# A graph layer pair on one core: TensorE's order within a step is changed, and drains carry its signals

## The reference

```python
def conv(x, W1, W2, src, dst, n):
    deg_out = clip(segment_sum(1, src), 1.0); deg_in = clip(segment_sum(1, dst), 1.0)
    norm = rsqrt(deg_out[src] * deg_in[dst])
    msg = (x[src] @ W1 + x[src] * x[dst] @ W2) * norm[:, None]
    return x @ W1 + segment_sum(msg, dst)
h = relu(conv(x, W1_1, W2_1))
h = conv(h, W1_2, W2_2)
out = layernorm(x + h)
```

## Time and profile before

| | |
|---|---|
| time, median of 3 runs | 1490.88 us (1488.17 to 1492.55) |
| span of the profiled execution | 1516.6 us (1.7% over the median of the runs) |
| mean granted TensorE clock in it | 0.757 of full speed |
| busy: PE / DVE / ACT / POOL | 998.5 / 978.8 / 741.3 / 795.9 us (66 / 65 / 49 / 52% of the span) |
| layer 0 / layer 1 in the span | steps from about 156 to 806 us / from 808 to 1515 us |

### The profile page before, as it was taken

The page is one execution under the profiler, slowest core; times in us unless marked ns, Lnnn a source line. Parts: engine busy times, 40 slices in busy tenths (PEclk is TensorE's granted clock), DMA queues, the critical chain, the costliest instruction groups (busy, mean ns, idle before and its releaser), DMA issues. The chain is left out here.

```text
span 1516.6 us, 33831 instructions
## 1 busy us (share of the span) xinstructions
PE 998.5 (66%) x13162; PEld 933.6 (62%) x13162; DVE 978.8 (65%) x2390; ACT 741.3 (49%) x2763; POOL 795.9 (52%) x813
## 2 busy tenths in 40 slices
PE   1775467666667666766783466767777667776676
PEld 1664356666666656766782366666666666666676
DVE  8577667565556655666583257767677767777676
ACT  3113145555555555655691145545554545555455
POOL 6575435555555555556205655655655555555540
PEclk9999567777777777667796667777787677777776
DMA  9854111122112211212112123333333233323322
GB/s 209 167 217 167 18 32 50 42 52 52 44 47 51 52 50 40 51 51 52 41 52 79 39 58 63 73 69 71 73 70 69 55 72 69 69 58 71 70 58 48
DMA packets 148693, 105.09 MB, mean 69 GB/s; under 512 B 115769, under 2 KB 128761, under 8 KB 147837
## 3 DMA queue, kind: packets, MB, share of 16 engines
q1 hardware_dynamic: 123176, 71.17, 17.8%
q0 software_dynamic: 25216, 32.50, 11.9%
q10 hardware_dynamic: 212, 0.42, 0.1%
HBM read 58.92 MB, written 45.11 MB: 69 GB/s over the span
## 5 line engine op out<-in xcount | busy, mean ns | idle before, releaser
L849 POOL DMA_INDIRECT c_rows<-table,k_row_i x394 | 380.3, 965 | 356.1 <-PE c_sum L882 159.7
L908 PE MATMUL c_out<-k_wcat,c_uvt 128*128 128x64 f32 x1516 | 319.6, 398 | 346.8 <-ACT c_uvt L990 309.5
L908 PEld LDWEIGHTS c_out<-k_wcat,c_uvt 128*128 128x128 f32 x1516 | 303.3, 306 | 373.3 <-ACT c_uvt L990 224.3
L849 POOL DMA_INDIRECT k_rows<-table,k_row_i x346 | 334.1, 966 | 294.5 <-PE c_sum L882 160.8
L990 ACT ACTIVATE c_uvt<-c_turn 128x512 f32<-128x512 f32 (+1 forms) x198 | 106.9, 590 | 539.2 <-remote 512.1
L1200 DVE TENSOR_TENSOR c_sum<-c_sum,c_own 128x512 f32<-128x512 f32 (+1 forms) x96 | 66.7, 695 | 381.9 <-remote 358.8
L882 PE MATMUL c_sum<-c_rows,c_sel 128*128 128x64 bf16 x4701 | 219.6, 221 | 48.2 <-issue 29.8
L882 PEld LDWEIGHTS c_sum<-c_rows,c_sel 128*128 128x128 bf16 x4701 | 219.3, 119 | 52.1 <-issue 50.3
L1141 DVE TENSOR_SCALAR c_sel<-k_place,k_grid 128x512 bf16<-128x512 f16 (+1 forms) x788 | 238.7, 371 | 0.0
L882 PE MATMUL c_sum<-c_yr,c_sel 128*128 128x64 bf16 x1567 | 209.6, 220 | 5.9 <-issue 4.4
L882 PE MATMUL c_sum<-c_rest,c_sel 128*128 128x64 bf16 x1567 | 207.8, 220 | 1.0 <-issue 1.0
(11 more groups left out here) (210 smaller groups left out, 1231.6 us busy)
## 6 DMA issues: line engine op xcount, KB each, us to landing
table<-c_y SPq DMA_DIRECT2D x47, 384.0 KB
out<-c_y SPq DMA_DIRECT2D x47, 256.0 KB
c_res<-in_x SPq DMA_DIRECT2D x46, 256.0 KB
table<-k_xh SPq DMA_DIRECT2D x4, 1820.0 KB
c_rows<-table,k_row_i POOLq DMA_INDIRECT x394
k_rows<-table,k_row_i POOLq DMA_INDIRECT x346
table<-k_xh SPq DMA_DIRECT2D x1, 3575.0 KB
table<-k_xh SPq DMA_DIRECT2D x1, 1040.0 KB
```

Source lines behind the costliest of these rows:

```text
L849: nc.gpsimd.indirect_dma_start(out=rows[:, b % RING, i], out_offset=None, in_=tables[l], in_offset=bass.IndirectOffsetOnAxis(ap=k.row_i[:, ...
L908: last = nc.tensor.matmul(out_bank(g)[:, n, :], uvt[:, g % 2, n, :], weights, start=True, stop=True)
```

## The change

TensorE's step becomes sums of s, transposes of group s - 1, product of group s - 2, counts. The consumers of the product move one step later on each engine: relu from s - 2 to s - 3, the split of its result (`rests`) from s - 3 to s - 4, centre from s - 2 to s - 3, vary and square from s - 3 to s - 4, deviate and normalize from s - 4 to s - 5, the stores from s - 3 - l to s - 4 - l. ACT's `turned_back` moves from the last place of step s to the first place of step s + 1, which is the same place in its queue. The ends of the layers are written out to match. Each increment that rode on the last matmul of a run in `add_up`, `count`, `multiply` and `turn_over` now rides on a drain of TensorE that follows the run. The matmuls of the degree lookups (L864), the lane transposes (L857) and the tally (L921) keep theirs.

```diff
-                for g in ended(s - 3 - l):
+                for g in ended(s - 4 - l):
                     store(g)
...
                         for q, part in enumerate(parts(b)):
-                            last = nc.tensor.matmul(p_sum[g % BANKS][:, t - GROUP[g][0], :], sel[:, b % 2, i, n * P:(n + 1) * P], part[:, i],
+                            nc.tensor.matmul(p_sum[g % BANKS][:, t - GROUP[g][0], :], sel[:, b % 2, i, n * P:(n + 1) * P], part[:, i],
                                                     start=first and q == 0, stop=q == 2, skip_group_check=True)
                     if i == BATCH[b] - 1 or i % HALF_BATCH == HALF_BATCH - 1:
-                        last.then_inc(summed, 1)
+                        pe.drain().then_inc(summed, 1)
...
-                last.then_inc(counted, 1)
+                pe.drain().then_inc(counted, 1)
...
-                last.then_inc(multiplied, 1)
+                pe.drain().then_inc(multiplied, 1)
...
-                last.then_inc(turned, 1)
+                pe.drain().then_inc(turned, 1)
...
                 if s == 1 and l == 0:
                     pe.wait_ge(k.lanes_back, EARLY)
-                for g in ended(s - 2):
-                    multiply(g, turn)
                 add_up(s, turn)
                 for g in ended(s - 1):
                     turn_over(g, turn)
+                for g in ended(s - 2):
+                    multiply(g, turn)
                 if s in COUNT_AT[l]:
                     count(COUNT_AT[l][s], turn)
...
             for s in STEPS:
+                for g in ended(s - 2):
+                    turned_back(g)
                 if l == 1:
-                    for g in ended(s - 3):
+                    for g in ended(s - 4):
                         square(g)
-                    for g in ended(s - 4):
+                    for g in ended(s - 5):
                         deviate(g)
                 for g in ended(s - 1):
                     scale(g)
...
                 if l == 0:
-                    for g in ended(s - 2):
+                    for g in ended(s - 3):
                         relu(g)
                 else:
-                    for g in ended(s - 4):
+                    for g in ended(s - 5):
                         normalize(g)
...
-                for g in ended(s - 1):
-                    turned_back(g)
+            turned_back(g0 - 1)
...
                 if l == 0:
-                    for g in ended(s - 3):
+                    for g in ended(s - 4):
                         rests(g)
...
                 if l == 1:
+                    for g in ended(s - 4):
+                        vary(g)
                     for g in ended(s - 3):
-                        vary(g)
-                    for g in ended(s - 2):
                         centre(g)
```

More of the change, by code:

```diff
@@ L831, in sync @@
                             fetch(g)
-                for g in ended(s - 3 - l):
+                for g in ended(s - 4 - l):
                     store(g)
-            for g in range(g0 - 2 - l, GROUPS):
+            for g in range(g0 - 3 - l, GROUPS):
                 store(g)
@@ L892, in count @@
                 for i in range(b - a):
-                    last = nc.tensor.matmul(k.p_count[:, 0:TILES], hot_l[:, :, i], hot_t[:, i], start=u == COUNTS[0][0] and i == 0,
+                    nc.tensor.matmul(k.p_count[:, 0:TILES], hot_l[:, :, i], hot_t[:, i], start=u == COUNTS[0][0] and i == 0,
                                             stop=True, skip_group_check=True)
-                last.then_inc(counted, 1)
+                pe.drain().then_inc(counted, 1)
             def multiply(g, turn=None):
@@ L907, in multiply @@
                 for n in range(wide(g)):
-                    last = nc.tensor.matmul(out_bank(g)[:, n, :], uvt[:, g % 2, n, :], weights, start=True, stop=True)
-                last.then_inc(multiplied, 1)
+                    nc.tensor.matmul(out_bank(g)[:, n, :], uvt[:, g % 2, n, :], weights, start=True, stop=True)
+                pe.drain().then_inc(multiplied, 1)
             def turn_over(g, turn=None):
@@ L915, in turn_over @@
                 for n in range(wide(g)):
-                    last = nc.tensor.transpose(turn_bank(g, n)[:, n % 4, :], uv[:, g % 2, n].rearrange("p a d -> p (a d)"), k.ident[:, :])
-                last.then_inc(turned, 1)
+                    nc.tensor.transpose(turn_bank(g, n)[:, n % 4, :], uv[:, g % 2, n].rearrange("p a d -> p (a d)"), k.ident[:, :])
+                pe.drain().then_inc(turned, 1)
             def tally():
@@ L1061, in scalar @@
                     A(root_up[:, :], k.degree[:, 8 * LOOKUPS[s]:8 * LOOKUPS[s] + 8], ACT.Sqrt).then_inc(k.root_found, 1)
-                for g in ended(s - 1):
-                    turned_back(g)
+            turned_back(g0 - 1)
             scale(g0)
             if l == 0:
+                relu(g0 - 2)
                 relu(g0 - 1)
@@ L1074, in scalar @@
             else:
+                square(g0 - 3)
+                deviate(g0 - 4)
+                normalize(g0 - 4)
                 square(g0 - 2)
@@ L1366, in vector @@
             if l == 0:
-                rests(g0 - 2)
+                rests(g0 - 3)
             select(b1)
             if l == 1:
+                deviate(g0 - 4)
+            products(g0)
+            if l == 1:
+                vary(g0 - 3)
+                centre(g0 - 2)
+            split_up(b1)
+            if l == 0:
+                rests(g0 - 2)
+            else:
                 deviate(g0 - 3)
-            products(g0)
-            split_up(b1)
-            if l == 1:
                 vary(g0 - 2)
```

## The result

The changed kernel takes 1758.9 us (median of 5 runs, 1755.8 to 1766.9), the kernel before beside it 1492.6 us: the ratio is 1.178 [1.175, 1.182]. I had said 1210 us, faster. It is slower by 18%, outside my range, and what came is my first rival, the drains that are held; its 1942 us was 183 us too high.

What follows compares the result with a forecast made beforehand. A chain through POOL's gather bursts, held signals, ACT and L908 was taken as the bound. With prompt drains, 1516.6 - 138 - 8 - 144 + 6 = 1233 us of span, a median of 1210; range 1145 to 1480.

Steps and rivals of the forecast that it cites:

- first rival: TensorE's drains beside POOL's gathers are held like the matmuls' signals: +5.4 us a step, median 1942 us; chance 0.19.
- The reading of the kernel before: POOL's gathers hold signals of finished matmuls; join L1200 starts 4.8 us and L990 3.9 us late in layer 1.
- The order: Output product L908 goes behind the transposes and leaves the chain, saving 1.15 + 3.66 us in the step read.
- A drain that isn't held: Each TensorE drain costs 0.35 us in lost overlap and restart: 1.5 us a step in layer 0, 1.7 in layer 1.
- Signals: If a TensorE drain's signal is prompt beside gathers, POOL is let go 4 to 5 us earlier in each step.
- 0.64: Chance given to the forecast's own range, 1150 to 1330 us, with TensorE's drains prompt beside gathers.
- a rival of 0.6 us a drain: TensorE's drains get out only in pauses between gathers: 2.9 us a step on TensorE, 1380 us; chance 0.13.
- the clock: TensorE, being fuller, should run near the silent stretch's clock of 0.95; above 0.85 was expected in the profile after.
- What would show each step wrong: Named beforehand: TensorE drains of several us, 1 us issue gaps behind each, or layer 1 steps above 12 us.

## Why the prediction was wrong

- **The reading of the kernel before was right.** Signals are held by POOL's gathers, and with loads in their place the same code runs at 8.1 and 9.4 us a step (I had read 7.3 us from the silent stretch). The experiments with loads show that it is the gathers, which I had only inferred.
- **The order: right in sign, too large in size.** L908 left the chain and TensorE's wait for L990 went to nothing. Alone it gives 4.4%, 68 us. I had counted 1.15 us and up to 3.66 us a step; measured are 1.3 us in layer 0, 0.6 us in layer 1. What I had left out is the creep of the sums, 311.6 us of standing where it was 37.0.
- **A drain that isn't held: I took 0.35 us, between 0.05 and 0.45.** It is 0.2 to 0.3 us: inside my bounds, below the value I took, and of no weight beside the holds.
- **The step that failed is "Signals": "If it is prompt, POOL is let go 4 to 5 us earlier in each step, and matmuls carry nothing that could be held."** The drain isn't prompt: in most steps it comes out when the signal did, 1.0 us behind the burst and 4.4 us behind the last sum (4.5 us before), and POOL waits as long as before. The argument that gave it 0.64 stood in the first rival: "matmuls without a signal ran unhindered beside gathers (45 in 2.56 us), so emptying TensorE is not itself held". These 45 were the start of a run; the next rows of the same group showed TensorE creeping with matmuls that carried no signal either. They spoke for a stall of all of TensorE's work, not of signals on matmuls alone, and then a drain is a place where the engine has to stand until the stall is over. I used those rows for a rival of 0.6 us a drain and not against the forecast.
- **The first rival came, at 17.0 us a step and not 19.** It had one hold too many: the turn's drain comes behind 8 matmuls in a fresh burst and is seldom held (11 us in all). The forecast also had the clock wrong: above 0.85 was said, 0.698 came. TensorE's busy time grew by 145 us, from 998.5 to 1143.4 us, with the same 13162 matmuls, nearly all of it in turn and counts behind the stop; how much of the 249 us that explains no run separates. That the stop itself lowers the clock is the reading nearest to the rows: with loads, where nothing stands, the clock is 0.92 to 0.99 in stretches in which TensorE is busy for 80 to 87%. The busy share alone doesn't sort it, for it is 65 to 67% with the clock at 0.698 (changed kernel), 0.757 (before) and 0.794 (order alone).
- **What would show each step wrong** was named and is what the profile shows: drains of several us, joins waiting for sums, steps above 12 us.

## What to carry to other kernels

An increment on a matmul lets TensorE run on while its signal is late; a drain in the same place turns the lateness into a stop. So before putting drains in, find out what makes signals late, and whether the engine had work under them. Here that is POOL's indirect gathers, and the version to keep is the new order with its increments on the matmuls, 0.956 of the time before. Where rows show a run of an engine at full speed and then a creep, both belong to the argument: the run at the start says only how far the engine gets ahead.

## What the runs showed of the hardware

- While POOL issues indirect gathers in a row, 0.94 us each with 0.30 us between, TensorE's matmuls run on for a few tens and then mostly get out one to three at a time, every 0.71 us or twice that; signals and drains behind them come out with them. It ends 1.0 to 1.1 us after the last gather at the latest. Plain loads from POOL, with the same packets and bytes on its queue, do nothing of it, nor do plain loads from SP (ratio 0.698 and 0.690), nor gathers one by one every 3.2 us.
- A drain of TensorE with nothing held lasts 0.02 us beyond the last matmul, and the next run starts 0.2 to 0.3 us behind it. A drain of POOL behind an indirect gather costs some 2.3 us.
- Of TensorE's run-ahead: it was 25 and 45 matmuls in the two rows shown, each with its weight load. PSUM — Partial Sum Buffer, section Engine vs sequencer instructions (the Trainium skill), gives TensorE a queue 64 deep, an estimated 32 matmuls with their loads; the rows lie on both sides of it, so it may be this queue that runs dry, but no run here shows it.
- PSUM — Partial Sum Buffer, section Engine vs sequencer instructions (the Trainium skill), puts the increment on the matmul itself and keeps a drain for a barrier by itself. The runs agree with the advice, though not with a prompt increment beside gathers: 0.956 without drains, 1.178 with them, in the same order.
